# A 64-step LSTM with a network of sign weights behind it: high parts of x a step earlier, weight pieces one a step, and eight output matmuls moved behind step 63

## The chip, the cores and the metric

One core of a Trainium2 chip runs the program. The metric is the device time of one execution in microseconds (us); lower is better. Three runs of the kernel before gave 279.79 to 280.56 us, median 280.08.

## The reference, cut to what matters

```python
# x: (32, 64, 256)   cond_1024: (32, 256)   Wx, Wh: (256, 1024)
xW = jnp.einsum('ntd,dg->ntg', x, Wx) + b
def step(carry, xw_t):                      # 64 steps, h0 = cond_1024, c0 = 0
    prev_h, prev_c = carry
    a = xw_t + prev_h @ Wh
    i, f, o = (sigmoid(a[:, 256*n:256*n+256]) for n in range(3))
    g = tanh(a[:, 768:])
    next_c = f * prev_c + i * g
    next_h = o * tanh(next_c)
    return (next_h, next_c), next_h
...
h = jnp.concatenate([h, -h], axis=-1)       # h: all 64 steps' hidden states
h = s0 * (h @ where(k0, 1, -1));  h = relu(h) * 2      # 512 -> 1024
h = s1 * (h @ where(k1, 1, -1));  h = relu(h) * 2      # 1024 -> 1024
h = s2 * (h @ where(k2, 1, -1))                        # 1024 -> 256
return x + h
```

## The kernel before, in words

Everything stays transposed: features on the 128 partitions, and (step, batch) on the free axis. Products that need full precision are made of a high and a low part of each operand.

**Input product.** x is cut along time into four quarters of 16 steps (512 columns). The kernel calls them x tiles (x, i, j): quarter i, gate block j of 8. A tile is six matmuls of 512 columns (line 420): high and low parts of x by high and low parts of Wx. `x_hi(i, k)` on ScalarE (line 509) makes the high part of half k of quarter i; `x_lo(i, k)` on VectorE (line 622) subtracts it from x for the low part. The parts lie in two buffers (quarter i in buffer i mod 2), so `x_hi(i, ...)` for i of 2 or more waits until all tiles of quarter i - 2 and those before are computed (`x_mm`). `x_empty` on ScalarE (line 518) moves a finished tile from PSUM to `xw`. Quarter 1's high parts are made on GpSimd.

**Recurrence.** Step t on TensorE is 16 matmuls of 32 columns (line 392, the high part of h) and 16 of 64 columns (line 401, low part). VectorE sums column pairs (line 730), ScalarE takes tanh of the gates (line 580), VectorE makes c (lines 736 to 741), ScalarE tanh(c) (line 585), VectorE h's high part (line 747) and then its low part (lines 748, 750). ScalarE writes the next step's seed into PSUM (line 526). Here "the tail of step t" is what ScalarE and VectorE do behind their own part of step t and in front of that of step t + 1; each engine runs its instructions in the order written.

**Network.** Its weights come as bytes and are turned into signed ones by `w0_make(0)`, `(1)`, `(2)` (lines 667, 669, 673), `w1_make` (line 678) and `w2_make` on VectorE, in the tails that W0_STEPS, W1_STEPS, W2_STEPS name. Layers 0 and 1 are tiles (layer, c, m): chunk c of steps (seven chunks, six of 8 steps with 256 columns, the last of 16 with 512), output block m. Line 437 is their matmul; ScalarE evicts the high part with relu (line 544), VectorE the low part (line 627). Four PSUM banks, WK0 to WK3, take x, layer 0 and layer 1 tiles in turn, and a tile waits for the low part of the tile that had its bank. Output tiles (o, c, k) (line 453) add block k of layer 1's result into ACC0 and ACC1, four matmuls each for chunks 0 to 5; `y_add(c, n)` on VectorE (line 634) adds the sum (c, n) to x, and SyncE sends it out.

**Order.** `tile_order` writes one order of all matmuls outside the recurrence. `make_plan` deals it out: behind each step t TensorE gets `pe_plan[t]`, the step's fill, of about the time that the recurrence needs; `act_plan[t]` and `dve_plan[t]` hold the evictions and sums of tail t. How much VectorE gets follows from the constants in the line with AHEAD: a running estimate `ahead` of how far the recurrence is in front of TensorE, capped at AHEAD. List 64 is all that is left behind the last step; its layer 0 tiles (0,6,n) need h's low part of step 63.

Of the kernel before, what the change touches and what calls it, by code (L numbers as in the profile page):

```python
# [20 lines left out]
NWK = 4  # L21
NH2 = 6
LAST = 2
WARM = 16


# [14 lines left out]
X_BANKS = (6, 7, 4, 5, 0, 1, 2, 3)  # L41
WX_GROUPS = ((0, 1), (1, 2), (2, 4), (4, 6), (6, 8))

X2_STEPS = (1, 2)
X3_STEPS = (4, 5)
W0_STEPS = (3, 3, 6)
W1_STEPS = (7, 8)
W2_STEPS = (15,)

KEPT = 4  # L50


STEP, CHAIN, CHAIN_MIN, LOW, SUM, AHEAD, KEEP = 0.87, 2.46, 2.87, 0.33, 0.40, 0.35, 0.05


def fill(t):
# [21 lines left out]
def sums(c):  # L78

    n = B * CHUNKS[c][1]  # L80
    return ((0, 0, n), (1, 0, n)) if c < NC - 1 else ((0, 0, n), (1, 0, n // 2), (1, n // 2, n))
# [6 lines left out]
def tile_order():  # L88

    def third(c, m):  # L90
        if c == NC - 1:
            return []
        at = (2, 2, 3, 4, 5, 6, 6, 7) if c == 0 else (0, 1, 2, 3, 4, 5, 6, 6)
        return [((0, c + 1, n), 4) for n in range(8) if at[n] == m]

    at_o = (5, 5, 6, 6, 7, 7)
    order = [(("x", i, j), 6) for i in (1, 2) for j in range(NJ)]
    for m in range(8):
        order += [(("x", 3, n), 6) for n in range(NJ) if (0, 1, 2, 3, 4, 5, 6, 8)[n] == m] + [((0, 0, m), 4)]
    order.append((("x", 3, 7), 6))  # L100
    for c in range(NC):
        for m in range(8):
            if m < 2 and c:
                order += [((1, c, m), 10 - 2 * m), (("o", c - 1, 6 + m), 4), ((1, c, m), 6 + 2 * m)]
            else:
                order.append(((1, c, m), 16))
            order += [(("o", c, k), 2 * len(sums(c))) for k in range(6 if c < NC - 1 else 8 - KEPT) if at_o[k] == m]
            if c < NC - 2:
                order += third(c, m)
        if c == NC - 2:  # L110
            rest = [(tile, 1) for tile, n in order[-LAST:] for _ in range(n)]
            del order[-LAST:]
            share = len(rest) // 8
            for n in range(8):
                order += [((0, c + 1, n), 4)] + rest[share * n:share * n + share]
            order += rest[8 * share:]

    kept = range(8 - KEPT, 8)
    return order + ([(("o", NC - 1, k), 2) for k in kept[:-1]] + [(("o", NC - 1, kept[0]), 2), (("o", NC - 1, 7), 2)]
                    + [(("o", NC - 1, k), 2) for k in kept[1:]] + [(("o", NC - 1, k), 2) for k in kept])  # L120
# [89 lines left out]
def lstm_ffn(nc, x_d, small_d, wx_d, wh_d, k0_d, k1_d, k2_d, out_d):  # L210
    ctx = ExitStack()
    with ctx:
# [126 lines left out]
        def wx_group(j):  # L339
            return sum(j >= j1 for _, j1 in WX_GROUPS)  # L340
# [35 lines left out]
        def _(eng):  # L376
# [97 lines left out]
            e.wait_ge(zeroed, 1)  # L474
            for n in range(WARM):
                eng.matmul(G[n % 2][:, 0:256], zero16[:, 0:128], zero16[:, 0:256], start=True, stop=True)  # L476
# [13 lines left out]
        def _(eng):  # L490
# [12 lines left out]
            def x_hi(i, k):  # L503
                if i == 0:
                    e.wait_ge(dx0[k], 16)
                else:
                    e.wait_ge(dx[i - 1], 16)
                    e.wait_ge(x_mm, NJ * (i - 1))
                eng.activation(xs[:, i % 2, 0, k, :], x[:, i, k], ACT.Copy).then_inc(xh)

            def x_empty(tile):
                _, i, j = tile
                e.wait_ge(x_mm, NJ * i + j + 1)
                e.wait_ge(biased, 2)
                if i == 3:
                    e.wait_ge(wxl, len(WX_GROUPS))
                    e.wait_ge(wlo, 4)
                eng.activation(xw[:, 4 * i:4 * i + 4, j], TILE[bank[tile]][:, :].rearrange("p (u c) -> p u c", c=128),  # L518
                               ACT.Identity, bias=biasS[:, j:j + 1], scale=2.0 if j < 2 else 1.0).then_inc(x_out)

            def seed(t, g):

                if t % 16 == 0:
                    wait_x_out(e, ("x", t // 16, 3 if t == 0 and g == 0 else 7))
                src = xw[:, t // 4, 4 * g:4 * g + 4].rearrange("p j (t b) -> p j t b", t=4)[:, :, t % 4]
                eng.activation(G[g][:, 0:256].rearrange("p (j h b) -> p j h b", h=2, b=B),  # L526
                               src.unsqueeze(2).broadcast_to((P, 4, 2, B)), ACT.Copy,
                               scale=half_x0 if t == 0 else half_x).then_inc(seeded[g])

            def layer_hi(tile):  # L530
                layer, c, m = tile
                e.wait_ge(l_mm[layer], 8 * c + m + 1)
                if layer == 0 and 2 <= c < NC - 1:
                    e.wait_ge(l_mm[1], 8 * (c - 1))
                if layer == 0 and c == NC - 1:
                    e.wait_ge(seeded[1], 16)
                if layer == 1 and m >= NH2:
                    e.wait_ge(o_mm, 7 * c + m - NH2 + 1)
                if layer == 1 and m < NH2 and c > 0:
                    if m + 8 - NH2 < 7:  # L540
                        e.wait_ge(o_mm, 7 * (c - 1) + m + 8 - NH2 + 1)
                    else:
                        e.wait_ge(acc_mm[1], c)
                eng.activation(layer_dst(tile, 0), layer_src(tile), ACT.Relu).then_inc(hi_made[layer])  # L544
# [32 lines left out]
            for t in range(T):  # L577
                for g, (j0, j1) in enumerate(GROUPS):
                    e.wait_ge(added[g], t + 1)
                    eng.activation(tT[:, B * j0:B * j1], aT[:, j0:j1].rearrange("p j b -> p (j b)"), ACT.Tanh,  # L580
                                   scale=half_gain0 if t == 0 else half_gain).then_inc(tanhed[g])
                if t + 1 < T:
                    seed(t + 1, 0)
                e.wait_ge(c_made, t + 1)
                eng.activation(tC[:, :, :].rearrange("p j b -> p (j b)"), cD[:, :], ACT.Tanh, scale=0.5).then_inc(c_tanh)  # L585
                if t + 1 < T:
                    seed(t + 1, 1)
                if t in X2_STEPS:
                    x_hi(2, X2_STEPS.index(t))
                if t in X3_STEPS:  # L590
                    x_hi(3, X3_STEPS.index(t))
                for tile in act_plan[t]:
                    if tile[0] == "x":
                        x_empty(tile)
                    else:
                        layer_hi(tile)
# [4 lines left out]
        def _(eng):  # L601
# [18 lines left out]
            def x_lo(i, k):  # L620
                wait_x_hi(e, i, k)
                eng.tensor_tensor(xs[:, i % 2, 1, k, :], x[:, i, k], xs[:, i % 2, 0, k, :].bitcast(F32),
                                  ALU.subtract).then_inc(xl)
# [19 lines left out]
            def signs():  # L643

                e.wait_ge(dsmall, 16)
                bits = sv[:, 0:3].bitcast(I32)
                eng.tensor_scalar(sign0[:, :].bitcast(I32), bits[:, 0:1], 31, SIGNS - (1 << 32), ALU.arith_shift_right,
                                  ALU.bitwise_and).then_inc(signed)
                eng.tensor_scalar(sign1[:, :].bitcast(I32), bits[:, 1:2], 31, SIGNS - (1 << 32), ALU.arith_shift_right,
                                  ALU.bitwise_and).then_inc(signed)  # L650
                eng.tensor_scalar(sc[:, 11:13].bitcast(I32), bits[:, 0:2], 0x7FFFFFFF, None, ALU.bitwise_and).then_inc(signed)
                e.wait_ge(signed, 3)
                eng.tensor_scalar(sign1[:, :].bitcast(I32), sign1[:, :].bitcast(I32), (SIGNS | ONE1) - (1 << 32), None,
                                  ALU.bitwise_xor).then_inc(signed)
                eng.tensor_tensor(sc[:, 14:15], sc[:, 11:12], sc[:, 12:13], ALU.mult).then_inc(signed)
                e.wait_ge(signed, 5)
                eng.scalar_tensor_tensor(sc[:, 15:16], sc[:, 14:15], 8.0 / (HS * S0 * S1), sv[:, 2:3], ALU.mult,
                                         ALU.mult).then_inc(signed)
                e.wait_ge(signed, 6)
                e.wait_ge(zeroed, 3)  # L660
# [65 lines left out]
            for t in range(T):  # L726
# [24 lines left out]
                if t == 0:  # L751
                    signs()
                if t in X2_STEPS:
                    x_lo(2, X2_STEPS.index(t))
                if t in X3_STEPS:
                    x_lo(3, X3_STEPS.index(t))
                for n in range(3):
                    if t == W0_STEPS[n]:
                        w0_make(n)
# [60 lines left out]
```

## Time and profile before

| | us |
|---|---|
| median of 3 runs | 280.08 |
| profiled execution | 279.52 |
| its span | 277.7 |
| TensorE busy | 273.4 |
| weight loads busy | 223.8 |
| VectorE busy | 203.2 |
| ScalarE busy | 157.8 |

Times in the trace are microseconds from the start of the span. Matmuls are pipelined, and their ends are modelled: for the pace of TensorE the starts of matmuls are read, not its busy time. The granted TensorE clock is full throughout. In a timeline row the first number is the start, the second the time covered, and equal instructions that follow one another are merged (x16 means sixteen). The steps 0 to 63 are told apart by the first matmul of line 392.

### The profile page before, as it was taken

The page shows a single profiled execution, that of the slowest core. Times are in us where ns is not written, and L with a number is a line of the kernel's source. Part 1 is how long each engine was busy: PE and PEld are TensorE (multiplying, and loading weights), DVE is VectorE, ACT ScalarE, POOL GpSimd, SP SyncE. Part 2 cuts the span into 40 slices and gives each one's busy share as a digit, 9 for nine tenths or more (in the row PEclk, how much of TensorE's full clock was granted, in tenths as well). Part 3 has the DMA queues.
Part 4 walks back from the last instruction along what each step waited for, and adds up shares of the span by engine and source line. Part 5 has one row for each costly group of instructions (what it writes and reads, how often), then busy time and mean ns, then how long its engine had stood idle before and what let it go on. Part 6 is the DMA issues. An engine that isn't in the chain of part 4 may idle for free.

```text
span 277.7 us, 8789 instructions
## 1 busy us (share of the span) xinstructions
PE 273.4 (98%) x3616; PEld 223.8 (81%) x3616; DVE 203.2 (73%) x750; ACT 157.8 (57%) x481; POOL 2.0 (1%) x10
## 2 busy tenths in 40 slices
PE   8999999999999999999999999999999999999996
PEld 5888777778999998999999998999999995544553
DVE  3877888878888888888888888888887876431103
ACT  4797787878565656555556565555665545311100
POOL 0100000000000000000000000000000000000000
PEclk9999999999999999999999999999999999999999
DMA  6970000000000000000000000000000100010002
GB/s 186 384 306 1 4 2 0 2 4 2 2 2 0 5 21 21 2 2 4 21 20 5 1 30 13 2 2 22 22 2 0 40 4 2 0 38 2 0 0 76
DMA packets 4791, 8.72 MB, mean 31 GB/s; under 512 B 656, under 2 KB 2704, under 8 KB 4624
## 3 DMA queue, kind: packets, MB, share of 16 engines
q1 hardware_dynamic: 4464, 7.64, 7.8%
q8 instruction: 28, 0.46, 0.7%
q10 hardware_dynamic: 288, 0.52, 0.6%
q14 instruction: 11, 0.09, 0.1%
HBM read 6.07 MB, written 2.10 MB: 29 GB/s over the span
## 4 chain that ended last, share of the span: by engine, by line
PE 93%; ACT 3%; DVE 2%; issue 0%; DVEq 0%; POOL 0%; POOLq 0%
PE WK L437 50%; PE WK L420 11%; PE G L401 10%; PE ACC L453 9%; PE G L392 9%; PE G L476 1%; PE G L420 1%; ACT tT L580 1%; PE ACC L420 1%; ACT xw L518 1%; PE G L453 1%; ACT tC L585 0%; DVE aT L730 0%; DVE uT L739 0%; DVE cD L741 0%
## 5 line engine op out<-in xcount | busy, mean ns | idle before, releaser
L437 PE MATMUL WK<-h,k 128*128 128x256 f16 (+1 forms) x992 | 125.6, 276 | 0.4 <-DVE h L750 0.4
L437 PEld LDWEIGHTS WK<-h,k 128*128 128x128 fp8e5 x992 | 93.6, 98 | 15.1 <-issue 2.6
L580 ACT ACTIVATE tT<-aT 128x128 f32<-128x128 f32 x126 | 39.0, 310 | 58.1 <-DVE aT L730 56.8
L627 DVE SCALAR_TENSOR_TENSOR h<-WK,h 128x256 f16<-128x256 f32 (+1 forms) x105 | 42.6, 440 | 25.0 <-ACT h L544 25.0
L730 DVE TENSOR_REDUCE aT<-G 128x128 f32<-128x256 f32 x128 | 48.1, 418 | 7.7 <-PE G L401 7.1
L544 ACT ACTIVATE h<-WK 128x256 f16<-128x256 f32 (+1 forms) x104 | 36.2, 387 | 28.8 <-PE WK L437 28.8
L526 ACT ACTIVATE G<-xw 128x256 f32<-128x256 f32 x126 | 46.6, 370 | 0.0
L420 PE MATMUL WK<-xs,wxs 128*128 128x512 f32 x168 | 43.5, 402 | 0.0
L401 PE MATMUL G<-h,w 128*128 128x64 f16 x1008 | 39.5, 192 | 0.0
L392 PEld LDWEIGHTS G<-h,w 128*128 128x128 f16 x1008 | 32.9, 96 | 5.8 <-DVE h L747 4.1
L392 PE MATMUL G<-h,w 128*128 128x32 f16 x1008 | 35.1, 176 | 0.1
L420 PEld LDWEIGHTS WK<-xs,wxs 128*128 128x128 f32 x168 | 30.2, 188 | 5.6
L453 PE MATMUL ACC<-h,k 128*128 128x256 f16 (+1 forms) x224 | 34.2, 280 | 0.0
L401 PEld LDWEIGHTS G<-h,w 128*128 128x128 f16 x1008 | 33.2, 97 | 0.0
L437 PE MATMUL WK<-xw,k 128*128 128x512 f16 x128 | 28.4, 379 | 0.0
L585 ACT ACTIVATE tC<-cD 128x64 f32<-128x64 f32 x64 | 16.4, 256 | 17.6 <-DVE cD L741 17.6
L453 PEld LDWEIGHTS ACC<-h,k 128*128 128x128 fp8e5 x224 | 21.4, 98 | 6.1 <-DVE h L627 0.2
L747 DVE TENSOR_TENSOR h<-oP,tC 128x64 f16<-128x64 f32 x64 | 14.4, 225 | 13.9 <-ACT tC L585 13.9
L437 PEld LDWEIGHTS WK<-xw,k 128*128 128x128 fp8e5 x128 | 12.5, 98 | 14.1
L739 DVE SCALAR_TENSOR_TENSOR uT<-tT,cD 128x64 f32<-128x64 f32 x63 | 14.2, 225 | 6.7 <-ACT tT L580 0.2
L518 ACT ACTIVATE xw<-WK,biasS 128x512 f32<-128x512 f32 x28 | 18.0, 676 | 0.2 <-PE WK L420 0.2
L736 DVE SCALAR_TENSOR_TENSOR vT<-tT 128x64 f32<-128x64 f32 x63 | 14.2, 226 | 2.8
(66 smaller groups left out, 133.1 us busy)
## 6 DMA issues: line engine op xcount, KB each, us to landing
out_y<-x SPq DMA_DIRECT2D x14, 128.0 KB, 1.8
x<-in_x SPq DMA_DIRECT2D x3, 512.0 KB, 8.5
xw<-in_wh SPq DMA_DIRECT2D x4, 256.0 KB, 6.0
k<-in_k SPq DMA_DIRECT2D x1, 1024.0 KB, 10.5
xw<-in_wx SPq DMA_DIRECT2D x3, 256.0 KB, 6.1
x<-in_x ACTq DMA_DIRECT2D x2, 256.0 KB, 3.6
k<-in_k SPq DMA_DIRECT2D x1, 512.0 KB, 7.9
xw<-in_wx SPq DMA_DIRECT2D x2, 128.0 KB, 3.2
```

The lines of the kernel that those rows point to most:

```text
L392: eng.matmul(G[g][:, 64 * (j - j0):64 * (j - j0) + B], w16[:, 1, j, k], hi[:, k], start=False, stop=False, skip_group_check=True)
L401: ins = eng.matmul(G[g][:, 64 * (j - j0):64 * (j - j0 + 1)], w16[:, 0, j, k], pair[:, k].rearrange("p a b -> p (a b)"), start=False, stop= ...
L420: ins = eng.matmul(TILE[bank[tile]][:, :], wxs[:, wp, j, k], xs[:, i % 2, xp, k], start=a == 0, stop=a == 5)
L437: ins = eng.matmul(layer_src(tile), w, rhs, start=a == 0, stop=last)
L453: ins = eng.matmul(sum_bank(n)[:, 0:c1 - c0], w2[:, k, 128 * mo:128 * mo + 128], h2[:, k % NH2, part, c0:c1], start=k == 0 and part == 0, ...
L518: eng.activation(xw[:, 4 * i:4 * i + 4, j], TILE[bank[tile]][:, :].rearrange("p (u c) -> p u c", c=128), ACT.Identity, bias=biasS[:, j:j + ...
L526: eng.activation(G[g][:, 0:256].rearrange("p (j h b) -> p j h b", h=2, b=B), src.unsqueeze(2).broadcast_to((P, 4, 2, B)), ACT.Copy, scale= ...
L544: eng.activation(layer_dst(tile, 0), layer_src(tile), ACT.Relu).then_inc(hi_made[layer])
L580: eng.activation(tT[:, B * j0:B * j1], aT[:, j0:j1].rearrange("p j b -> p (j b)"), ACT.Tanh, scale=half_gain0 if t == 0 else half_gain).th ...
L585: eng.activation(tC[:, :, :].rearrange("p j b -> p (j b)"), cD[:, :], ACT.Tanh, scale=0.5).then_inc(c_tanh)
L627: eng.scalar_tensor_tensor(layer_dst(tile, 1), layer_src(tile), 0.0, layer_dst(tile, 0), ALU.max, ALU.subtract).then_inc(lo_made[tile[0]])
L730: eng.tensor_reduce(aT[:, j0:j1], G[g][:, 0:256].rearrange("p (j h b) -> p j b h", h=2, b=B), op=ALU.add, axis=AX.X).then_inc(added[g])
```

## The change

The high parts of quarters 2 and 3 are made in the tail of the step before the one in which their low parts are made: tails 0 and 1 for quarter 2, tails 3 and 4 for quarter 3 (before: 1 and 2, 4 and 5). The low parts stay in tails 1, 2, 4 and 5. `w0_make(0)` goes from tail 3 to tail 0, behind the small instructions that make the signs. The cap AHEAD is 0.30, not 0.35. And the eight matmuls of the output tiles (o,5,4) and (o,5,5), of which one stood behind each tile (0,6,n), stand together in front of (0,6,0).

With the changed numbers the lists of `make_plan` come out the same except for these: fill 63 has 23 matmuls for 19 (the four of (o,5,4) behind the 16 of (1,5,7)), list 64 begins with the four of (o,5,5), then the 32 of (0,6,0) to (0,6,7) with nothing between; the sum (c, n) = (0,1) goes from VectorE's tail 25 to tail 26, and (4,1) from tail 59 to tail 60. The banks and who had them before stay.

```diff
 LAST = 2
+FIRST = 8
 WARM = 16
...
-W0_STEPS = (3, 3, 6)
+W0_STEPS = (0, 3, 6)
...
-STEP, CHAIN, CHAIN_MIN, LOW, SUM, AHEAD, KEEP = 0.87, 2.46, 2.87, 0.33, 0.40, 0.35, 0.05
+STEP, CHAIN, CHAIN_MIN, LOW, SUM, AHEAD, KEEP = 0.87, 2.46, 2.87, 0.33, 0.40, 0.30, 0.05
...
             rest = [(tile, 1) for tile, n in order[-LAST:] for _ in range(n)]
             del order[-LAST:]
+
+            order += rest[:FIRST]
+            del rest[:FIRST]
             share = len(rest) // 8
             for n in range(8):
                 order += [((0, c + 1, n), 4)] + rest[share * n:share * n + share]
...
-                if t in X2_STEPS:
-                    x_hi(2, X2_STEPS.index(t))
-                if t in X3_STEPS:
-                    x_hi(3, X3_STEPS.index(t))
+                if t + 1 in X2_STEPS:
+                    x_hi(2, X2_STEPS.index(t + 1))
+                if t + 1 in X3_STEPS:
+                    x_hi(3, X3_STEPS.index(t + 1))
```

## Rows read from the trace of the kernel before

**Rows 1.** The page, the chain that ended last: shares of the span by engine.

```profile
PE 93%; ACT 3%; DVE 2%; issue 0%; DVEq 0%; POOL 0%; POOLq 0%
```

**Rows 2.** Windows between steps' first matmuls: length, busy us (instructions), clock, DMA, GB/s.

```profile
25.45:28.72 3.27, 3.27 (x43) 2.65 (x42) 2.66 (x10) 2.98 (x9) 0.00 (x0) 1.00 0.02 5
...
32.09:35.61 3.52, 3.43 (x43) 2.65 (x43) 3.08 (x12) 2.03 (x7) 0.00 (x0) 1.00 0.00 0
35.61:38.98 3.37, 3.37 (x42) 2.65 (x42) 2.73 (x11) 3.08 (x9) 0.00 (x0) 1.00 0.00 0
...
107.72:110.82 3.10, 3.10 (x54) 2.73 (x53) 2.67 (x12) 2.25 (x9) 0.00 (x0) 1.00 0.00 1
164.44:167.70 3.26, 3.22 (x55) 2.74 (x52) 2.86 (x12) 2.06 (x8) 0.00 (x0) 1.00 0.12 40
```

**Rows 3.** Timeline of step 63 and behind it: start us, us, engine, line, instruction.

```profile
227.96 0.56 PE L392 MATMUL G<-h,w 128*128 128x32 f16 x16
...
228.80 0.76 DVE L730 TENSOR_REDUCE aT<-G 128x128 f32<-128x256 f32 x2 [0.71 <-PE G L401]
...
229.16 1.91 PE L437 MATMUL WK<-h,k 128*128 128x256 f16 x16
...
231.13 0.22 DVE L750 TENSOR_TENSOR h<-h 128x64 f16<-128x64 f32 x1
...
231.50 1.02 PE L437 MATMUL WK<-h,k 128*128 128x512 f16 x4 [0.43 <-DVE h L750]
...
232.47 1.03 PE L437 MATMUL WK<-h,k 128*128 128x512 f16 x4
...
233.19 0.69 DVE L627 SCALAR_TENSOR_TENSOR xw<-WK,xw 128x512 f16<-128x512 f32 x1 [1.17 <-ACT xw L544]
```

**Rows 4.** Timeline, VectorE in the tail of step 0 (last sign instruction, next reduce).

```profile
22.52 0.16 DVE L657 SCALAR_TENSOR_TENSOR sc<-sc,small 128x1 f32<-128x1 f32 x1
...
23.11 0.76 DVE L730 TENSOR_REDUCE aT<-G 128x128 f32<-128x256 f32 x2 [0.43 <-PE G L401]
```

**Rows 5.** Timeline, VectorE in the tail of step 3: the two weight pieces.

```profile
32.34 0.68 DVE L667 TENSOR_TENSOR k<-k 128x512 uint32<-128x512 uint32 x1
...
32.94 0.54 DVE L669 TENSOR_SCALAR k<-k,seven,sign 128x512 uint32<-128x512 uint32 x1
```

**Rows 6.** Timeline, step 1's tanh(c) and its tail on ScalarE and VectorE.

```profile
24.77 0.26 ACT L585 ACTIVATE tC<-cD 128x64 f32<-128x64 f32 x1 [0.27 <-DVE cD L741]
...
25.05 0.23 DVE L747 TENSOR_TENSOR h<-oP,tC 128x64 f16<-128x64 f32 x1 [0.21 <-ACT tC L585]
...
25.24 0.62 ACT L509 ACTIVATE xs<-x 128x512 fp32r<-128x512 f32 x1
...
25.76 1.25 ACT L518 ACTIVATE xw<-WK,biasS 128x512 f32<-128x512 f32 x2
...
25.89 0.69 DVE L622 TENSOR_TENSOR xs<-x,xs 128x512 fp32r<-128x512 f32 x1 [0.21 <-ACT xs L509]
...
26.49 0.75 DVE L730 TENSOR_REDUCE aT<-G 128x128 f32<-128x256 f32 x2
26.95 0.64 ACT L580 ACTIVATE tT<-aT 128x128 f32<-128x128 f32 x2
```

**Rows 7.** Issue of the load of x's third quarter, and its time to landing.

```profile
7.27 0.51 SPq L363 DMA_DIRECT2D x<-in_x  x1
...
x<-in_x SPq DMA_DIRECT2D x1, 512.0 KB, 8.5
```

**Rows 8.** Timeline, VectorE in tails 25 and 26: h's high part and the next reduce.

```profile
103.84 0.22 DVE L747 TENSOR_TENSOR h<-oP,tC 128x64 f16<-128x64 f32 x1 [0.21 <-ACT tC L585]
...
105.49 0.75 DVE L730 TENSOR_REDUCE aT<-G 128x128 f32<-128x256 f32 x2
...
107.41 0.23 DVE L747 TENSOR_TENSOR h<-oP,tC 128x64 f16<-128x64 f32 x1 [0.22 <-ACT tC L585]
...
108.61 0.75 DVE L730 TENSOR_REDUCE aT<-G 128x128 f32<-128x256 f32 x2
```

## Prediction

> **What bounds the kernel now.** I read the page first: TensorE holds 93% of the chain that ended last [rows 1]. So only time in which TensorE's instruction stream stands still can be won, and a later VectorE or ScalarE instruction costs only where TensorE runs out of other work. To find such places I cut the span at the first matmul of each LSTM step (line 392) and took the periods as windows [rows 2]. A step whose fill is ten x matmuls takes 3.27 us when TensorE sets the pace (the one from 25.45; three more, from 18.89, 22.17 and 42.35, are within 0.01 of it). The step from 35.61 takes 3.37 with the same ten matmuls, and so do those from 28.72 and 38.98; the one from 32.09 takes 3.52. These four are too long by 0.10, 0.25, 0.10 and 0.10 us: there the recurrence, not TensorE, sets the pace. All later steps up to 63 have the length of their fill, but for a few tenths; the one from 107.72 (3.10) and the one from 164.44 (3.26) have 20 fill matmuls and are both paced by the recurrence.
>
> The second place is behind step 63. The 16 matmuls of tile (1,5,7) start at 229.16 and take 1.91 with the last one's modelled end; the stream advances by 0.108 us a 256-column matmul, so it is free at 229.16 + 16 x 0.108 = 230.89 (a fill of 22 or 23 of them lengthens its step by that much for each). The next matmul starts at 231.50, 0.15 after the end of h's low part (231.13 + 0.22) [rows 3]. That is 0.61 us of standing still.
>
> **Part 1: weights' first piece, moved from step 3 to step 0 (VectorE).** In step 0's tail VectorE runs the sign instructions to 22.52 + 0.16 = 22.68 and then waits until the reduce of step 1 at 23.11 [rows 4]. The piece takes 0.68, and the next instruction started 0.60 behind its start [rows 5]. With 0.04 from one dependent instruction to the next it starts at 22.72 and the reduce at 23.32: I take +0.20 us on the recurrence. Bounds: 0 (nothing if it could hide whole in the 0.43 of idle, which is shorter than the piece) and +0.29 (the whole 0.68).
> The Trainium skill, "VectorE: DVE Perf Modes", section "The DRAIN you can't avoid", says the next VectorE op doesn't start until the pipe is empty (and elsewhere on the page that an op which isn't held starts earlier). By the first sentence the reduce would be 0.29 late, the sum below 0.09 smaller, and the time 279.34; the 0.60 of the row speaks for the second.
>
> What of this reaches TensorE: h of step 1 would be at 25.05 + 0.20 = 25.25 [rows 6]; where nothing else holds it, a step's first matmul follows h by 0.31 (107.41 to 107.72, [rows 2, 8]), so step 2's matmuls start at 25.56 for 25.45: 0.11 lost. In step 1's tail ScalarE has one high part (0.62) and two x evictions (1.25) between tanh(c) at 24.77 and the next tanh at 26.95, with no idle time [rows 6]. The change leaves exactly this load there (high part of k=1 in place of k=0), so the next tanh is still 2.18 behind tanh(c): 27.15. Step 3's matmuls start at 28.92 for 28.72: the full 0.20 is lost here.
>
> **Part 2: high parts one step ahead (ScalarE), low parts where they were (VectorE).** Now the low part waits for the high part of the same tail: high part 25.24 to 25.86, low part 25.89, reduce 26.49 [rows 6]. After the change it can start behind h's low part, about 0.54 behind h, and frees VectorE 1.14 behind h. Loads of ScalarE by tail, before: steps 1, 2, 4, 5 one high part and two evictions each. After: step 0 one and one, step 1 one and two, step 3 one and one, step 4 one and two, steps 2 and 5 only two evictions. A recurrence hindered by nothing takes at most 3.10 us (the window from 107.72), under TensorE's 3.27. So steps 3 and 6 (tails 2 and 5 in front) fall to 3.27. Step 5 (tail 4 in front) keeps ScalarE's loop of 3.37 from tanh(c) to tanh(c), but a step paced by TensorE stands in front of it, behind which the recurrence is 3.27 - 3.10 = 0.17 early, and 3.37 - 0.17 = 3.20 is under 3.27. Nothing is added: the same four copies of 0.62 on the same engine. Their inputs are there: x's third quarter was issued at 7.27 and landed 8.5 later, at 15.8, and is first wanted at 21.6 [rows 7]; the fourth quarter is issued one us later and wanted ten later. The piece leaving step 3's tail takes 0.60 from VectorE (0.54 stays), so that the reduce of the 3.52 step comes at its natural place: 3.27.
>
> Sum of the front: step 3 starts at 28.92 (before 28.72), then five steps of 3.27: 32.19, 35.46, 38.73, 42.00, 45.27, against 45.61 before. **Gain 0.34 us.** Without step 0's delay it would be 0.54; with 0.29 of it, 0.25. The later steps are paced by TensorE and keep it.
>
> **Part 3: AHEAD 0.30.** Followed through, the planner's lists differ in two places: sum (0,1) goes from step 25's tail to step 26's, (4,1) from 59's to 60's. In tail 25 the reduce came 105.49 - 103.84 = 1.65 behind h, in tail 26 without the sum 108.61 - 107.41 = 1.20 [rows 8]. Afterwards h of step 26 is 0.31 earlier, at 107.10 (its reduce comes 0.84 behind the step's first matmul, as it does in step 63 (227.96 to 228.80, [rows 3]), and no longer 105.49 - 104.34 = 1.15), and the reduce 1.60 to 1.65 behind it, at 108.70 to 108.75 for 108.61. The step from 107.72 is paced by the recurrence, so step 28 starts 0.09 to 0.14 later: **loss 0.12 us.** The step from 164.44 has exactly this list and took 3.26 for 3.10 [rows 2], which bounds it at 0.16; below, 0. Steps 60 and 61 are TensorE's (23 fill matmuls, 0.28 more than the 3.10 of the recurrence): the moved sum lies beside them, nothing. Both results are wanted by matmuls over 2 us later, and the output's transfer is not near the end.
>
> **Part 4: eight last-layer matmuls together in front of layer 0's last chunk.** Four go behind tile (1,5,7) into step 63's fill, four to the head of the last list. 8 x 0.108 = 0.86 us: the stream goes on from 230.89 to 231.76, when h's low part has been ready since 231.35. Layer 0 starts 0.26 later than before but its eight tiles take 4 x 0.216 each and no interleaved 0.108 (tile starts were 231.50 and 232.47 [rows 3]), so the next layer starts at 231.76 + 6.91 = 238.67 for 239.28: **gain 0.61 us**, all of the standing still. Cover for the denser tiles: a tile's low part is done 2.38 us behind its first matmul (233.19 + 0.69 - 231.50), and its bank is wanted 3.46 behind (four banks): slack 1.08. VectorE, the slower of the two that empty it, takes 0.69 a tile, under the 0.86. The inputs of the eight (high and low parts of tiles (1,5,4), (1,5,5)) are done in step 61's tail. Bounds: 0.43 (the idle time that the profile itself puts down to h's low part, if the rest is a start-up cost that stays) and 0.61.
>
> **Sum.** 0.34 - 0.12 + 0.61 = 0.83 us. The profiled execution took 279.52 (span 277.7): 278.69. The median of the runs is 280.08, 0.56 above it; 0.83 less is 279.25, which I predict. Runs of one kernel spread by some tenths (279.79 to 280.56), so less than 0.3%, 0.84 us, can hardly be told from no change. The forecast lies on that line.
>
> **Rivals.**
> - *Front gives nothing (0.14).* ScalarE's list alone already explains the 3.37 (tanh without idle time); if its load binds wherever a high part and two evictions meet, and step 0's delay of 0.20 is followed by more, the front only breaks even: 280.08 - 0.49 = 279.6. Against: tails 2 and 5 lose their high part.
> - *The gap behind step 63 isn't filled (0.08).* Banks or evictions pace layer 0's tiles at the old 0.97 us: the start 0.26 later stays and the end term turns to -0.26. Sum 0.34 - 0.12 - 0.26 = -0.04: 280.1. Against: VectorE has 0.69 to do in each 0.97 now. If only the start-up part stays (0.43 for 0.61), 279.4.
> - *Moves without cost (0.12).* First piece hidden and the sum's move free: 0.54 + 0.61 = 1.15, 278.9.
> - *Slower (0.03).* The high part of x's fourth quarter in step 3's tail waits for all matmuls of the second quarter; the last of them are the first five of step 3's own fill, so the reserve shrinks from a step to about 1 us (they end by about 28.92 + 0.9 + 5 x 0.24 = 31.0, ScalarE comes near 31.9). Were they late, the next tanh stands behind the copy in ScalarE's queue and each us beyond the reserve costs one. From 1 + 0.83 + 0.84, some 2.7 us late, the kernel is slower: 281 or more. The fill of the step shows no such delay.
> - Forecast: 0.63.
>
> **Numbers.** The forecast's own range is 279.0 to 279.5 (front 0.25 to 0.54, middle 0 to 0.16, end 0.43 to 0.61). With the first rival and the cheap one, and a median of few runs moving by 0.2 or so, 278.7 to 279.9 holds 8 in 10. Faster by over 0.3%: half of the forecast and the cheap case, 0.44; within: 0.52; slower: 0.04.
>
> **What would show it.** Periods of the steps from about 32.2 on: 3.27 four times, none of 3.37 or 3.52; the reduce of step 1 at 23.3 and step 3's matmuls at 28.9. The period of step 27 at 3.19 to 3.26. No gap behind step 63's fill, layer 0's tiles 0.86 apart. A TensorE wait for a bank (low part of the tile four back), a ScalarE wait for x matmuls in step 3's tail, or a low part of x that holds the reduce beyond 0.9 us would prove me wrong.

## The result and the profile after

The changed kernel took 279.13 us (median of 22 runs, 278.55 to 280.39), the kernel before 280.24 in runs beside them. The ratio is 0.9963, 95% interval 0.9955 to 0.9971: 1.04 us less, 0.8 to 1.3. That is inside the range, on the side of "faster by over 0.3%" (the interval's end, 0.29%, lies just across that line), and 0.2 more than the 0.83 of the sum, which the interval just takes in.

The page of the changed kernel, its head, and the last chain's shares:

```profile
span 277.3 us, 8789 instructions
...
PE 273.6 (99%) x3616; PEld 224.5 (81%) x3616; DVE 203.7 (73%) x750; ACT 157.6 (57%) x481; POOL 2.0 (1%) x10
...
PE 99%; DVE 0%; DVEq 0%; issue 0%; POOL 0%; POOLq 0%
```

TensorE's share of the last chain went from 93% [rows 1] to 99%: the stretches in which the chain ran through ScalarE and VectorE are nearly gone. But the span fell by 0.4 us only, from 277.7, where the runs fell by 1.0. The difference lies in the start-up, which the prediction hadn't looked at. These are the making of a high part of Wx on ScalarE and the first matmuls of the second part of the input product, kernel before and then kernel after:

```profile
4.59 0.42 ACT L496 ACTIVATE wxs<-xw 128x256 fp32r<-128x256 f32 x1 [0.37 <-DMA xw<-in_wx]
...
7.76 2.90 PE L420 MATMUL ACC<-xs,wxs 128*128 128x512 f32 x12
```

```profile
4.84 0.42 ACT L501 ACTIVATE wxs<-xw 128x256 fp32r<-128x256 f32 x1 [0.57 <-DMA xw<-in_wx]
...
8.30 2.88 PE L425 MATMUL ACC<-xs,wxs 128*128 128x512 f32 x12
```

In this execution the matmuls came 0.54 us later, and with them step 0 (19.41 for 18.89). ScalarE waits here for a piece of Wx from memory, which came 0.25 us later; the 12 matmuls of the first part, in front of those shown, need it. How 0.25 becomes 0.54 was not followed; the next piece of Wx was not late (its high part starts at 5.97 for 6.86). In the two profiles with the latest step 0 (e1 and e8 below) it is that next piece: its high part starts at 8.17 and 8.28. The ten profiles of this study, in which the instructions up to there are the same, have step 0 anywhere from 18.82 to 20.25, so one execution's span says little here. I compare from step 0's first matmul on: 277.3 - 19.41 = 257.9 for 277.7 - 18.89 = 258.8, a gain of 0.9 us. From there on two executions agree to 0.04 us in each step that the kernels have in common.

Windows between the first matmuls of steps, after, from steps 1, 2, 4, 5 and 27, and then from step 63 to layer 0's last chunk and through that chunk's eight tiles (columns as in [rows 2]):

```profile
22.70:26.07 3.37, 3.37 (x43) 2.65 (x43) 2.86 (x13) 2.07 (x8) 0.00 (x0) 1.00 0.00 0
26.07:29.35 3.28, 3.28 (x43) 2.66 (x43) 2.69 (x11) 3.01 (x9) 0.00 (x0) 1.00 0.01 2
...
32.63:35.91 3.28, 3.28 (x44) 2.66 (x43) 2.59 (x11) 2.56 (x8) 0.00 (x0) 1.00 0.01 2
35.91:39.18 3.27, 3.27 (x43) 2.65 (x43) 2.71 (x11) 3.00 (x9) 0.00 (x0) 1.00 0.00 0
107.84:111.04 3.20, 3.20 (x54) 2.72 (x52) 2.80 (x12) 2.05 (x8) 0.00 (x0) 1.00 0.12 41
228.19:232.00 3.81, 3.81 (x61) 3.51 (x59) 2.66 (x12) 1.30 (x5) 0.00 (x0) 1.00 0.02 4
232.00:238.91 6.91, 6.91 (x35) 3.14 (x33) 4.43 (x8) 4.18 (x7) 0.00 (x0) 1.00 0.00 0
```

The 3.52 and the 3.37s of [rows 2] are 3.27 or 3.28 now; a new 3.37 stands at step 1; step 27 went from 3.10 to 3.20. The start of step 8 moved from 26.72 behind step 0 to 26.32: front, 0.40 gained. The profiles of e5 and e7 below, which have the same front, have step 8 at 26.28: so it is 0.40 to 0.44. Step 27 gives back 0.10. From step 63 to the first matmul of layer 1 it is 3.81 + 6.91 = 10.72 for 239.28 - 227.96 = 11.32: 0.60 gained. Together 0.90, the whole difference in these two profiles.

The front in the timeline after: the end of the signs, the moved weight piece, and the tails of steps 0 and 1.

```profile
23.05 0.16 DVE L662 SCALAR_TENSOR_TENSOR sc<-sc,small 128x1 f32<-128x1 f32 x1
...
23.25 0.69 DVE L672 TENSOR_TENSOR k<-k 128x512 uint32<-128x512 uint32 x1
...
23.85 0.75 DVE L735 TENSOR_REDUCE aT<-G 128x128 f32<-128x256 f32 x2
...
25.50 0.26 ACT L590 ACTIVATE tC<-cD 128x64 f32<-128x64 f32 x1 [0.28 <-DVE cD L746]
...
25.79 0.23 DVE L752 TENSOR_TENSOR h<-oP,tC 128x64 f16<-128x64 f32 x1 [0.22 <-ACT tC L590]
...
26.33 0.68 DVE L627 TENSOR_TENSOR xs<-x,xs 128x512 fp32r<-128x512 f32 x1
...
26.93 0.75 DVE L735 TENSOR_REDUCE aT<-G 128x128 f32<-128x256 f32 x2
...
27.63 0.50 ACT L585 ACTIVATE tT<-aT 128x128 f32<-128x128 f32 x2
...
28.68 0.26 ACT L590 ACTIVATE tC<-cD 128x64 f32<-128x64 f32 x1 [0.27 <-DVE cD L746]
```

The reduce of step 1 is 23.85 - 22.70 = 1.15 behind the step's matmuls for 23.11 - 22.17 = 0.94: 0.21 late. x's low part (26.33) starts 0.54 behind h's high part and no longer waits for ScalarE. Then read the last three: the reduce of step 2 is early, ScalarE takes it up 0.70 later (0.46 is usual), since it still evicts x tiles, but the two tanhs cover 0.50 us together and not 0.64. From tanh(c) to tanh(c) it is 28.68 - 25.50 = 3.18, not the 3.37 that I had taken for ScalarE's loop.

Behind step 63, after:

```profile
231.13 1.04 PE L458 MATMUL ACC<-h,k 128*128 128x256 f16 x8
...
231.35 0.23 DVE L755 TENSOR_TENSOR h<-h 128x64 f16<-128x64 f32 x1
...
232.00 7.07 PE L442 MATMUL WK<-h,k 128*128 128x512 f16 x32
```

The eight output matmuls cover the time in which nothing ran and 0.26 us more, and all 32 of layer 0 follow without a wait for a bank.

### The profile page after: what moved, and what is told of

The parts are those of the page before. It is cut to its first block, busy times and chain, and to the rows that moved or that the text cites. A ratio compares the mean times of both kernels' runs of the same rounds, so it can differ in the third digit from the quotient of the medians.

```text
span 277.3 us, 8789 instructions
## 1 busy us (share of the span) xinstructions
PE 273.6 (99%) x3616; PEld 224.5 (81%) x3616; DVE 203.7 (73%) x750; ACT 157.6 (57%) x481; POOL 2.0 (1%) x10
## 4 chain that ended last, share of the span: by engine, by line
PE 99%; DVE 0%; DVEq 0%; issue 0%; POOL 0%; POOLq 0%
PE WK L442 50%; PE WK L425 14%; PE G L406 11%; PE ACC L458 9%; PE G L397 9%; PE G L425 1%; PE G L481 1%; PE ACC L425 1%; PE G L458 1%; DVE x L639 0%; DVEq L217 0%; POOL zero L776 0%; POOL mx L777 0%; POOLq L814 0%; POOL seven L778 0%
## 5 line engine op out<-in xcount | busy, mean ns | idle before, releaser
L458 PE MATMUL ACC<-h,k 128*128 128x256 f16 (+1 forms) x224 | 33.1, 280 | 0.0
```

Of the source, the lines that this page charges most:

```text
L458: ins = eng.matmul(sum_bank(n)[:, 0:c1 - c0], w2[:, k, 128 * mo:128 * mo + 128], h2[:, k % NH2, part, c0:c1], start=k == 0 and part == 0, ...
```

## The experiments

All periods are read as above, from step 0's first matmul on, and compared with the kernel before unless said otherwise.

**Each part alone.** Four kernels, each the kernel before with one part of the change.

e1, high parts only, those of X3_STEPS in the same way:

```diff
-                if t in X2_STEPS:
-                    x_hi(2, X2_STEPS.index(t))
+                if t + 1 in X2_STEPS:
+                    x_hi(2, X2_STEPS.index(t + 1))
...
```

> Only the high parts of x go one step ahead; both weight pieces stay in step 3's tail, AHEAD 0.35, output matmuls interleaved. Theory (terms add up; the low part's wait for the high part made the 3.37 us steps): the steps that took 3.37 fall to 3.28, step 1 stays 3.28, the step behind the two weight pieces stays too long but shrinks from 3.52 to about 3.35 since h comes earlier against TensorE. Steps 1 to 7 gain 0.40 to 0.47 us, as much as in the full change without moving a piece; ratio about 0.9985. Rival (ScalarE's load of one high part and two evictions made them): steps 2 and 5 in front of it unchanged at 3.37, gain 0.2 or less. Second rival (the weight piece carried the front's gain): gain near 0.15.

Ratio 0.9986 (0.9971 to 1.0001). Windows from steps 3 to 6:

```profile
29.97:33.24 3.27, 3.27 (x43) 2.65 (x43) 2.72 (x11) 2.61 (x8) 0.00 (x0) 1.00 0.02 5
33.24:36.57 3.33, 3.33 (x44) 2.66 (x43) 2.93 (x11) 2.36 (x8) 0.00 (x0) 1.00 0.01 2
36.57:39.82 3.25, 3.25 (x43) 2.65 (x43) 2.67 (x11) 2.98 (x9) 0.00 (x0) 1.00 0.00 0
39.82:43.10 3.28, 3.28 (x43) 2.66 (x43) 2.81 (x12) 2.76 (x8) 0.00 (x0) 1.00 0.02 5
```

Step 8 starts 26.25 behind step 0 for 26.72: 0.47 gained, by this part alone at least as much as by the whole front of the change (0.40, and 0.44 in e5 and e7). Even with both weight pieces in step 3's tail the step behind them takes 3.33, not 3.52, because h is early: its high part starts at 32.75, 0.49 ahead of step 4's matmuls, for 0.29 before (31.80 and 32.09).

Which cause made the 3.37s can't be read from steps 3 and 6, where ScalarE lost a high part too, nor from step 2, which took 3.27 before. Step 5 tells them apart. ScalarE has the same high part and two evictions in front of it as before, and the 3.33 in front leaves no lead; still it takes 3.25 for 3.37. Its reduce and tanhs:

```profile
37.42 0.75 DVE L730 TENSOR_REDUCE aT<-G 128x128 f32<-128x256 f32 x2
...
38.12 0.50 ACT L580 ACTIVATE tT<-aT 128x128 f32<-128x128 f32 x2
```

The low part's wait for the high part made the 3.37 there; ScalarE's load alone did not.

e2, the weight piece only:

```diff
-W0_STEPS = (3, 3, 6)
+W0_STEPS = (0, 3, 6)
```

> Only the first weight piece goes from step 3's tail to step 0's. Theory: step 1 takes 3.37 for 3.28 (reduce 0.2 late), the steps with a low part waiting for a high part stay 3.37, the 3.52 step falls to about 3.27 to 3.30; sum a gain of 0.05 to 0.15 us, which the run times can't tell from none. Rival (the piece carries the front's gain): 0.25 us or more, no step becomes longer.

Ratio 0.9986 (0.9976 to 0.9996). Windows from steps 1, 2, and 4 to 6:

```profile
22.73:26.10 3.37, 3.37 (x43) 2.65 (x43) 2.86 (x13) 1.55 (x7) 0.00 (x0) 1.00 0.00 0
26.10:29.47 3.37, 3.37 (x43) 2.66 (x43) 2.72 (x11) 3.08 (x9) 0.00 (x0) 1.00 0.01 5
...
32.84:36.12 3.28, 3.28 (x44) 2.66 (x43) 2.77 (x12) 2.25 (x7) 0.00 (x0) 1.00 0.00 0
36.12:39.39 3.27, 3.27 (x43) 2.65 (x42) 2.63 (x10) 2.98 (x9) 0.00 (x0) 1.00 0.00 0
39.39:42.67 3.28, 3.28 (x44) 2.66 (x43) 2.67 (x10) 2.98 (x9) 0.00 (x0) 1.00 0.03 5
```

0.21 gained, where I expected 0.05 to 0.15. Step 1 loses 0.09 as expected, and step 2, in front of which a low part waits for its high part, loses 0.10. The miss is in steps 5 and 6: I had them stay at 3.37. But behind step 4, at TensorE's pace, h is 0.2 early (it starts 0.49 ahead of step 5's matmuls, at 35.63), and the next two late low parts use this up (0.39 and 0.30 ahead of steps 6 and 7). So alone the piece is worth 0.21; on top of the high parts it is worth 0.40 - 0.47 = -0.07, or -0.03 with the 0.44 of e5 and e7, which is nothing clear of the 0.04 by which profiles differ. Both parts win the same slack, and the piece brings its price at step 1.

e3, only AHEAD 0.30 (one number in its line):

> Only AHEAD 0.30. Theory: step 27 takes 3.20 for 3.10, all others the same: 0.10 us lost. Rival (a later sum frees the recurrence somewhere): some step between 25 and 28 or 59 and 62 gets shorter by over 0.02, gain.

Ratio 1.0006 (0.9987 to 1.0024), which can't tell a loss from none; the trace can. Windows from steps 26 and 27:

```profile
105.39:108.77 3.38, 3.38 (x58) 3.12 (x56) 2.94 (x13) 2.38 (x10) 0.00 (x0) 1.00 0.03 5
108.77:111.97 3.20, 3.20 (x54) 2.72 (x52) 2.80 (x12) 2.05 (x8) 0.00 (x0) 1.00 0.12 41
```

3.20 for 3.10, every other step the same within 0.03, none of them clearly shorter: 0.10 lost.

e4, only the eight output matmuls:

```diff
             del order[-LAST:]
+            order += rest[:8]
+            del rest[:8]
             share = len(rest) // 8
```

> Only the eight output matmuls in front of layer 0's last chunk. Theory (they fill 0.61 us of standing still): from step 63's first matmul to layer 0's first 3.81 for 3.54 us, its eight tiles 6.91 for 7.78, together 0.60 gained; all steps before it as before; ratio about 0.9978. Rival (banks or evictions pace the tiles): tiles stay near 7.7, a loss of 0.2.

Ratio 0.9988 (0.9976 to 1.0000); expected 0.9978, just inside. The timeline has step 63, layer 0's chunk and layer 1's first matmuls:

```profile
227.88 0.55 PE L394 MATMUL G<-h,w 128*128 128x32 f16 x16
...
231.70 7.07 PE L439 MATMUL WK<-h,k 128*128 128x512 f16 x32
238.60 2.32 PE L439 MATMUL WK<-xw,k 128*128 128x512 f16 x10
```

10.72 behind step 63 for 11.32: 0.60 gained. All steps before are as before. The rival falls.

From step 0 to the end of the span the four parts alone are worth 0.47, 0.21, -0.13 and 0.60 us, 1.15 together, where the whole change has 0.89: what is missing is, but for a few hundredths, the slack that the first two share.

**e5: half of them in the gap.** The changed kernel with FIRST = 4; the other four come behind the eighth tile.

> The changed kernel with four output matmuls in front of layer 0's last chunk (in step 63's fill) and the other four behind its eighth tile. Theory (only what covers the standing still is gained): TensorE is free 3.37 us behind step 63's first matmul and still waits for h's low part until 3.54; eight tiles in 6.91, four output matmuls in 0.43: layer 1 begins 10.88 us behind step 63's first matmul, against 11.32 before and 10.72 in the changed kernel. Rival (dense tiles are what is gained, not the fill): 10.7 as in the changed kernel.

One execution, 279.53 us. Its timeline:

```profile
228.50 0.56 PE L397 MATMUL G<-h,w 128*128 128x32 f16 x16
...
231.44 0.60 PE L458 MATMUL ACC<-h,k 128*128 128x256 f16 x4
231.95 7.08 PE L442 MATMUL WK<-h,k 128*128 128x512 f16 x32
238.87 0.60 PE L458 MATMUL ACC<-h,k 128*128 128x256 f16 x4
239.30 2.32 PE L442 MATMUL WK<-xw,k 128*128 128x512 f16 x10
```

Layer 1 begins 10.80 behind step 63, between the 10.72 of eight and the 11.32 of none: what counts is the time covered, not the dense tiles. It is 0.08 less than expected: layer 0 starts at 3.45 and not at 3.54. Here h's low part ends at 231.89, and the first matmul that needs it starts 0.06 later; behind 0.61 us of standing still it was 0.15 [rows 3]. So 0.09 us of the 0.61 was such a start-up delay, and the eight matmuls of the change win it too.

**e6: ScalarE's load out of step 1's tail.** The changed kernel with both high parts of quarter 2 in step 0's tail.

```diff
-                if t + 1 in X2_STEPS:
-                    x_hi(2, X2_STEPS.index(t + 1))
+                if t == 0:
+                    x_hi(2, 0)
+                    x_hi(2, 1)
```

> The changed kernel with both high parts of x's third quarter in step 0's tail, so that step 1's tail has only two evictions on ScalarE. Theory (ScalarE delays step 2's first tanh by 0.24 us, and the pair of tanhs catches up 0.14 of it): distance from the reduce to the first tanh 0.46 for 0.70, from there to h 1.48 for 1.34, step 2's period 3.28 as now; step 1 stays 3.37, since VectorE's piece makes that. Nothing gained. Rival (ScalarE's load in tail 0 binds): step 1 takes more than 3.40.

ScalarE around step 2's tanhs:

```profile
26.03 1.25 ACT L523 ACTIVATE xw<-WK,biasS 128x512 f32<-128x512 f32 x2
27.44 0.64 ACT L585 ACTIVATE tT<-aT 128x128 f32<-128x128 f32 x2 [0.16 <-DVE aT L736]
```

The tanhs wait for the reduce again, cover 0.64, and h comes 1.48 behind the first for 1.34. Steps 1 and 2 take 3.36 and 3.25 (3.37 and 3.28 in the changed kernel, 3.36 and 3.25 in e5, whose front is that of the changed kernel), and step 8 comes 26.28 behind step 0, as in e5 and e7: nothing gained, one execution 279.13 us. The 0.24 by which ScalarE is late is caught up by 0.14 and for the rest hidden.

**e7: the sums put in front of long fills.** The changed kernel, AHEAD back at 0.35, and

```diff
+    for y, t0, t1 in ((("y", 0, 1), 25, 27), (("y", 2, 1), 43, 44)):
+        dve[t0].remove(y)
+        dve[t1].append(y)
     return pe, act, dve, bank, before
```

> The changed kernel with AHEAD back at 0.35 and two output sums put by hand in front of the steps with 25 fill matmuls: sum (0,1) in step 27's tail, (2,1) in step 44's. Theory (a sum in the tail in front of a step of 20 fill matmuls holds the recurrence there): step 27 takes 3.06 to 3.10 for 3.20, step 44 3.06 to 3.10 for 3.26, steps 28 and 45 keep 3.60: 0.26 to 0.34 us less than the changed kernel. Rival (the sum only moves its delay): steps 28 and 45 grow by 0.1 or more, nothing gained.

278.77 us for 279.98, ratio 0.9953 (0.9939 to 0.9967). Windows from steps 27, 28, 44 and 45:

```profile
107.82:110.88 3.06, 3.06 (x55) 2.73 (x52) 2.50 (x11) 2.06 (x8) 0.00 (x0) 1.00 0.00 0
110.88:114.48 3.60, 3.60 (x59) 3.32 (x58) 3.15 (x13) 2.13 (x8) 0.00 (x0) 1.00 0.11 36
164.50:167.55 3.05, 3.05 (x54) 2.73 (x52) 2.54 (x11) 2.05 (x8) 0.00 (x0) 1.00 0.00 0
167.55:171.16 3.61, 3.61 (x60) 3.32 (x59) 3.16 (x13) 2.14 (x8) 0.00 (x0) 1.00 0.13 41
```

3.06 for 3.20 and 3.05 for 3.26, and the steps of 25 fill matmuls take what they took: 0.35 us less than in the changed kernel's profile by these two steps, 0.31 less than in e5's (3.19 and 3.23). The intervals of the ratios, 0.9939 to 0.9967 here and 0.9955 to 0.9971 for the changed kernel, overlap; it is the traces that show this gain.

**e8: half a piece in step 0's tail.** As e7, and `w0_make(0)` on columns 0 to 255 in tail 0, on the rest in tail 3 in front of `w0_make(1)`, which waits for it:

```diff
-                    eng.tensor_tensor(a, a, b, ALU.bitwise_xor).then_inc(w0_made)
+                    half = slice(0, 256) if n == 0 else slice(256, 512)
+                    eng.tensor_tensor(a[:, half], a[:, half], b[:, half], ALU.bitwise_xor).then_inc(w0_made)
...
-                    if t == W0_STEPS[n]:
+                    if t == (0, 3, 6, 3)[n]:
```

> As e7_sums_placed, and the first weight piece cut in two: half of its columns in step 0's tail, half in step 3's. Theory (the whole piece is longer than the idle time in tail 0, half fits): step 1 takes 3.28 for 3.37, step 4 keeps 3.28; steps 0 to 7 gain 0.47 to 0.49 on the kernel before for the 0.40 of the changed one; with the sums 0.35 to 0.43 us less than the changed kernel, ratio to before about 0.9950. Rival (any VectorE work in tail 0 delays step 1's reduce by its whole length): step 1 still 3.33 or more.

278.60 us for 279.98, ratio 0.9946 (0.9932 to 0.9959). The half piece and the reduce behind it, and the window from step 1:

```profile
24.07 0.42 DVE L676 TENSOR_TENSOR k<-k 128x256 uint32<-128x256 uint32 x1
24.42 0.75 DVE L740 TENSOR_REDUCE aT<-G 128x128 f32<-128x256 f32 x2
```

```profile
23.53:26.81 3.28, 3.28 (x44) 2.66 (x43) 2.74 (x14) 2.25 (x8) 0.00 (x0) 1.00 0.00 0
```

Step 1 takes 3.28; step 8 starts 26.22 behind step 0: 0.50 gained on the kernel before, for 0.40 in the changed kernel's profile and 0.44 in e7's. It has the lowest median of all, though its interval overlaps those of e7 and of the changed kernel, and only the traces (0.06 us by step 8) put it in front of e7. Its profiled execution had the latest step 0 of all (20.25) and a span of 277.7, as long as that of the kernel before: the start-up hides in one execution what the rest has gained (1.36 us from step 0 on).

## Why the prediction was right

The forecast case came true, with the right sign and place for each term: front 0.40 for 0.34, middle -0.10 for -0.12, end 0.60 for 0.61; 0.90 for 0.83 from step 0 on. The remaining 0.1 to the runs' 1.04 is inside their interval. That the time itself, 279.13, lies only 0.12 from the 279.25 is in part luck: the base of 280.08, from three runs, was 0.16 under the 280.24 of the 22 beside the changed kernel. And the bounds of the three terms give a gain of 0.52 to 1.15, which is 278.9 to 279.6, a little wider than the range of 279.0 to 279.5 written for them.

- **Piece to step 0.** Right to 0.01: reduce 0.21 late for 0.20, 0.04 to start it, 0.60 from its start to the next instruction. By the sentence of the Trainium skill, "VectorE: DVE Perf Modes", section "The DRAIN you can't avoid", that the next op does not start until the pipe is empty, it would have been 0.29. The reduce at 23.85 starts before the piece's end at 23.94, so the trace goes with the page's other sentence, on an op that is not held. As part of the whole the move was no gain: e1 has 0.47 without it. That it pays only without the move of the high parts the prediction did not say; half a piece (e8) has no price at step 1.
- **ScalarE's loop.** This step was mis-sized. "The full 0.20 is lost here", because the next tanh would be 2.18 behind tanh(c) and everything after it as far behind as ever. The tanh did come late (27.63 - 25.50 = 2.13), but with both reduces done by then the pair of tanhs takes 0.14 less. h's high part then ended at 29.20, 0.15 ahead of step 3's matmuls, where 0.06 is enough: TensorE set step 2's pace and lost no more than the 0.10 of step 1, 0.11 up to step 3 (9.94 behind step 0 for 9.83). Of these 0.09, the five periods behind, 16.38 for the 16.35 of the sum, took back a part. The front was 0.06 too low, 0.10 by the profiles of e5 and e7.
- **High parts ahead.** Right: the low part starts 0.54 and the reduce 1.14 behind h (25.79, 26.33, 26.93), as worked out. e1 shows that this part carries the front, and its rival (ScalarE alone makes the 3.37) falls by step 5. The loop of 3.37 from tanh(c) to tanh(c) that the prediction leaves to ScalarE in tail 4 was not there either: 3.18 in tail 1 here, 39.18 - 35.99 = 3.19 in tail 4 of e1. Before, both ends met: the low part's wait gave the tanh at 26.95, and so did ScalarE's list. Idle time of zero in front of an instruction didn't mean that its engine set the pace.
- **AHEAD.** Right in place and sign, 0.10 inside the 0.09 to 0.14 (e3): the reduce of step 27 comes 0.99 behind the step's first matmul (107.84 to 108.83), for the 0.98 to 1.03 worked out. Step 44 proved a good model for step 27: e7 takes the delay away in both.
- **The gap.** 0.60 of 0.61, by e4 and e5, and 3.81 + 6.91 as worked out. The lower bound, 0.43, did not apply: nothing of a start-up cost stays when TensorE doesn't stand still.
- **Rivals.** The wait of step 3's high part for x matmuls did not appear: step 4 takes 3.28. Nor did the moves come without cost: step 1 takes 3.37 and step 27 3.20. The start-up's spread was missing from the range's reasons; it moves single executions by over a microsecond, more than the whole change.

## What to carry to other kernels

On a kernel whose main engine is full, cut the trace at a repeated instruction and price each period against its fill: every tenth of a microsecond was to be found this way, and each edit's worth could be read from one profile, to about 0.04 us, where run times could not tell it. Price edits that aim at neighbouring stalls together: slack made by one covers the other, and here two gains of 0.47 and 0.21 gave 0.40 to 0.44. Put side work in front of the longest fills, cut it to the idle time it goes into, and keep independent work for the place where a chain ends last.

## What the runs showed of the hardware

- A ScalarE pair that is late catches up: two tanhs of 0.31 cover 0.50 us when both inputs lie ready (the changed kernel and e1) and 0.64 when the second waits for its own (e6), 0.14 of a 0.24 delay.
- A matmul that waits for VectorE started 0.06 us behind the write's end when TensorE had stood still for under 0.1 us (e5), and 0.15 behind it after 0.61 us [rows 3]. It isn't any standing still that does it: in the kernel before, step 5's first matmul (35.61) also starts 0.06 behind h's high part, after TensorE has stood still for 0.25 us. What makes the 0.15 was not told apart.
- In ten profiles, one of each kernel, with the same instructions up to there, the recurrence starts anywhere between 18.82 and 20.25 us; the waits for pieces of Wx from memory differ from one to the next.
